# Attention's buffers in the place of the expert weights, 11 weight halves loaded early, and ScalarE's Gelu table asked for early

## The reference

```
x = layernorm(x + self_attention(x))        # 16 heads of 64, causal, with a projection
x = layernorm(x + cross_attention(x, ctx))  # 16 heads of 16, 77 context rows, one mask
x = layernorm(x + moe(x))
# moe: logits = x @ Wr.T; softmax; the two best of 8 experts, weights normalised;
#   for each expert e, in order: tokens of e up to a capacity of 1280;
#     the ones beyond it take the fallback FFN instead (fw1, fb1, fw2, fb2)
#   y += w * (gelu(x_e @ W1[e] + b1[e]) @ W2[e] + b2[e])   # exact gelu, 256 -> 1024 -> 256
```

## Time and profile before

| | |
|---|---|
| median of three runs | 1456.32 us |
| profiled execution | 1455.44 us, its span 1453.7 us |
| TensorE busy | 1288.9 us (89%), granted clock 0.96 on average |
| VectorE / ScalarE / GpSimd busy | 1081.1 / 922.0 / 731.8 us |
| attention block | 0 to 958.4 us |
| routing block | 958.4 to 1012.1 us |
| experts, final block | 1012.1 to 1401.6, 1401.6 to 1453.7 us |
| DMA | 208.96 MB, of which the 18 weight loads 18.9 MB |

### The profile page before, as it was taken

How to read it: one execution, slowest core, us unless ns; L and a number is a source line. 1 busy time by engine, 2 the same in 40 slices (tenths; PEclk the granted TensorE clock), 3 DMA queues, 4 the chain that set the end, 5 groups by cost and what they waited for, 6 DMA issues and landing times. The chain is left out here.

```text
span 1453.7 us, 47504 instructions
## 1 busy us (share of the span) xinstructions
PE 1288.9 (89%) x16821; PEld 1081.1 (74%) x16821; DVE 1081.1 (74%) x3112; ACT 922.0 (63%) x2383; POOL 731.8 (50%) x974
## 2 busy tenths in 40 slices
PE   4899999999999999999999998736999999999930
PEld 3788888887888888888888887513788888888820
DVE  4898899888888988988988988566455555555537
ACT  4677878777787887887888776304444444444436
POOL 4435666565566566566566453411243434444326
PEclk9999999999999999999999999965999999999975
DMA  9756767776776776767777654068233363333345
GB/s 242 132 101 137 160 148 188 166 155 150 200 158 144 204 154 156 180 172 154 159 197 160 130 112 76 23 253 338 61 70 80 102 164 75 74 74 75 70 157 201
DMA packets 292449, 208.96 MB, mean 144 GB/s; under 512 B 218782, under 2 KB 249630, under 8 KB 289792
## 3 DMA queue, kind: packets, MB, share of 16 engines
q1 hardware_dynamic: 278784, 180.87, 52.2%
q0 software_dynamic: 7136, 18.76, 4.5%
q10 hardware_dynamic: 6304, 6.29, 1.5%
HBM read 93.79 MB, written 65.93 MB: 110 GB/s over the span
## 5 line engine op out<-in xcount | busy, mean ns | idle before, releaser
L1784 PE MATMUL ps_e<-xt,wres 128*128 128x128 f16 x3408 | 343.4, 220 | 6.1 <-DMA xt<-xg 5.1
L1784 PEld LDWEIGHTS ps_e<-xt,wres 128*128 x3408 | 284.9, 98 | 78.3 <-issue 6.8
L1848 ACT ACTIVATE act_g<-ps_e,b 128x128 f32<-128x128 f32 x568 | 161.8, 368 | 208.6 <-PE ps_e L1784 208.6
L1791 PE MATMUL ps_e<-wres,g_hi 128*128 x568 | 214.6, 379 | 0.8 <-DVE g_lo L1871 0.8
L753 ACT ACTIVATE probs<-st_k,nmax 128x128 f32<-128x128 f32 (+1 forms) x512 | 202.3, 452 | 17.3 <-DVE nmax L1003 17.3
L1751 POOL DMA_INDIRECT z_scr<-e_y,dst_i x71 | 85.1, 1198 | 210.2 <-DVE e_y L1862 206.9
L1003 DVE CUSTOM_DVE_ANT_0 st_k<-ps,causal 128x128 f32<-128x128 f32 (+1 forms) x512 | 160.7, 351 | 31.9 <-ACT probs L753 16.5
L760 ACT ACTIVATE pt_hi<-ps 128x384 f16<-128x384 f32 x256 | 124.9, 488 | 59.1 <-PE ps L460 57.1
L1320 POOL TENSOR_TENSOR o_st<-o_norm,o_st 128x256 f16<-128x256 f32 x128 | 86.0, 672 | 149.7 <-ACT o_st L768 149.5
L1793 PE MATMUL ps_e<-wres,g_lo 128*128 x568 | 154.9, 273 | 0.0
L1008 DVE TENSOR_TENSOR pt_lo<-ps,pt_hi 128x384 f16<-128x384 f32 x256 | 140.9, 550 | 16.8 <-ACT pt_hi L760 15.6
(11 more groups left out here) (285 smaller groups left out, 3981.7 us busy)
## 6 DMA issues: line engine op xcount, KB each, us to landing
k_pair<-k_pair SPq DMA_DIRECT2D x96, 256.0 KB, 6.4
st_p<-in_moe_w SPq DMA_DIRECT2D x24, 768.0 KB, 6.7
w_scr<-st_p SPq DMA_DIRECT2D x24, 768.0 KB, 5.0
wres<-w_scr SPq DMA_DIRECT2D x18, 1024.0 KB, 22.7
v_scr<-v_tok SPq DMA_DIRECT2D x32, 512.0 KB, 4.3
v_pos<-v_scr SPq DMA_DIRECT2D x64, 256.0 KB, 6.1
q_st<-st_q SPq DMA_DIRECT2D x64, 128.0 KB, 2.8
z_scr<-zero SPq DMA_DIRECT2D x32, 256.0 KB, 5.2
```

What stands on the lines that cost most here:

```text
L1784: last = mm(out, w(c * FF + f * P, b, P), xt[:, t % X_BUFS, a, c], start=(m == 0), stop=(m == 5))
L1791: mm(out[:, 0:2 * D], g_hi[:, t % G_BUFS, f], w(KC * FF + f * D, 0, 2 * D), start=(f == 0), stop=False, skip_group_check=True)
L1848: nc.scalar.activation(act_g[:, k % 2, f], ps[:, 3 + 2 * (k % 2) + f // 4, (f % 4) * P:(f % 4 + 1) * P], ACT.Gelu, bias=bias[:, f:f + 1], ...
```

## The change

- The tensor wres (18 halves of 8 KB a partition, WSIZE = 4096 float16) is allocated before attention and stays. Attention's large buffers become views of it. In halves 0 to 10 (FRONT = 11) lie wqk (0, 1), wv (2), stage_p (3, 4), k_pair (5, 6), q_st (7), v_tok (8) and wp (9, 10); behind half 10 lie, by `kept`, w2, stage, stage_x, probs, o_st and o_t, which are in use to the end of attention.
- SP's queue in attention gets the loads of halves 0 to 10, in three parts: 0 to 4 in step 31, once all pieces are in w_scr and all fills are done; 5 to 8 in step 32, once all self-attention scores are computed and the last values have been stored; 9 and 10 once the last projection is done. The routing block loads halves 11 to 17.
- Attention's filler matmul reads w2["q"], since wv may be overwritten by then.
- ScalarE's queue of the experts block begins with one activation with Gelu on a single column, whose result is unused.

```diff
--- before.py
+++ after.py
@@ -57,6 +57,7 @@
 PAIRS = H // 2
 
 ZERO_STEPS = TILES
+FRONT = 11
 V_LOADS = 2
 
 V_FILLS, K_FILLS = 3, 4
@@ -77,10 +78,27 @@
         return ctx.enter_context(nc.semaphore(name))
 
 
-    wqk = {n: sb("w2_" + n, [P, 2, KC, PAIRS, 2, HS], F16) for n in "qk"}
-    wv = sb("wv_pair", [P, 2, KC, H * HS], F16)
-    wp = sb("proj_pair", [P, 2, H, D], F16)
-    w2 = {n: sb("xw_" + n, [P, 2, KC, D], F16) for n in ("q", "k", "v", "o")}
+    wres = keep["wres"]
+    taken = [FRONT * WSIZE]
+
+    def early(first, n, dims, **sizes):
+        return wres[:, first * WSIZE:(first + n) * WSIZE].rearrange("p (%s) -> p %s" % (dims, dims), **sizes)
+
+    wqk = {n: early(at, 1, "k c i x d", k=2, c=KC, i=PAIRS, x=2) for at, n in enumerate("qk")}
+    wv = early(2, 1, "k c n", k=2, c=KC)
+    stage_p = wres[:, 3 * WSIZE:5 * WSIZE].bitcast(F32).rearrange("p (h d) -> p h d", h=H)
+    k_pair = early(5, 2, "s l a t i", s=2, l=2, a=2, i=PAIRS)
+    q_st = early(7, 1, "s g a t i", s=2, g=2 * GROUPS, a=2, i=PAIRS)
+    v_tok = early(8, 1, "s h k d", s=2, h=H, k=2)
+    wp = early(9, 2, "k h d", k=2, h=H)
+    expert_rows = weight_rows(io)
+
+    def kept(n, dt, dims, **sizes):
+        at = taken[0]
+        taken[0] += n * (2 if dt is F32 else 1)
+        return wres[:, at:taken[0]].bitcast(dt).rearrange("p (%s) -> p %s" % (dims, dims), **sizes)
+
+    w2 = {n: kept(2 * KC * D, F16, "k c d", k=2, c=KC) for n in ("q", "k", "v", "o")}
     wr = sb("wr", [P, KC, E], F32)
     proj_b = sb("proj_b", [P, D], F32)
     ident = keep["ident"]
@@ -95,9 +113,8 @@
 
 
 
-    stage = {n: sb("st_" + n, [P, KC, D * 4], F32) for n in "vkq"}
-    stage_p = sb("st_p", [P, H, D], F32)
-    stage_x = {n: sb("st_x" + n, [P, KC, D], F32) for n in ("k", "v", "q", "o")}
+    stage = {n: kept(KC * D * 4, F32, "c n", c=KC) for n in "vkq"}
+    stage_x = {n: kept(KC * D, F32, "c n", c=KC) for n in ("k", "v", "q", "o")}
     ld = {n: sem("ld_" + n) for n in ("v", "k", "q", "p", "x")}
     s_small, s_hi, s_lo, s_const = sem("s_small"), sem("s_hi"), sem("s_lo"), sem("s_const")
 
@@ -127,20 +144,17 @@
     x_nat = sb("x_nat", [P, 2, D], F32)
     x_hi = sb("x_hi", [P, 2, KC, P], F16)
     x_lo = sb("x_lo", [P, 2, KC, P], F16)
-    q_st = sb("q_st", [P, 2, 2 * GROUPS, 2, GTOK // 2, PAIRS], F16)
     q_low = stage["q"][:, 0, 0:P * PAIRS // 2].bitcast(F16).rearrange("p (b t i) -> p b t i", t=GTOK // 2, i=PAIRS)
-    k_pair = sb("k_pair", [P, 2, 2, 2, P, PAIRS], F16)
-    v_tok = sb("v_tok", [P, 2, H, 2, HS], F16)
     v_pos = sb("v_pos", [P, 2, 2 * GROUPS, 1 + 2 * HS], F16)
     nmax = sb("nmax", [P, 2, 2], F32)
     masked = stage["k"][:, 0, 0:2 * 384].rearrange("p (g n) -> p g n", g=2)
-    probs = sb("probs", [P, 2, 384], F32)
+    probs = kept(2 * 384, F32, "g n", g=2)
     rden = sb("rden", [P, 4], F32)
     pt_hi = sb("pt_hi", [P, 2, 384], F16)
     pt_lo = sb("pt_lo", [P, 2, 384], F16)
     o_norm = sb("o_norm", [P, 2, 4, HS], F32)
-    o_st = sb("o_st", [P, 2, 2 * GROUPS, 2, HS], F16)
-    o_t = sb("o_t", [P, P, H], F16)
+    o_st = kept(2 * 2 * GROUPS * 2 * HS, F16, "s g k d", s=2, g=2 * GROUPS, k=2)
+    o_t = kept(P * H, F16, "t h", h=H)
     x_bias = sb("x_bias", [P, D], F32)
     y1 = sb("y1", [P, D], F32)
     y2 = sb("y2", [P, D], F32)
@@ -349,6 +363,11 @@
             sp.wait_ge(s_x2_lo, t + 1)
             sp.dma_start(io["pair_scr"][bass.ds(t * P, P), :], x2_pair[:, p].rearrange("p k d -> p (k d)")).then_inc(s_out_pair[p], 16)
 
+        def expert_weights(first, last):
+            for n in range(first, last):
+                at = slice(n * WSIZE, (n + 1) * WSIZE)
+                sp.dma_start(wres[:, at], expert_rows[:, at]).then_inc(keep["s_w"][n // 2], 16)
+
         def step(s):
             if s == -3:
                 load_x(0)
@@ -378,6 +397,16 @@
                 query_move(s + 1)
                 query_low_first(s + 1)
                 query_low_second(s + 1)
+            if s == TILES - 1:
+                sp.wait_ge(s_w_out, 16 * (PIECES + 1))
+                sp.wait_ge(s_fill, NF * TILES)
+                expert_weights(0, 5)
+            if s == TILES:
+                sp.wait_ge(s_scores, GROUPS * TILES)
+                sp.wait_ge(s_v_out, 16 * TILES)
+                expert_weights(5, 9)
+                sp.wait_ge(s_proj, TILES)
+                expert_weights(9, FRONT)
             if has(s - 2):
                 x2_out(s - 2)
                 pair_out(s - 2)
@@ -405,7 +434,7 @@
 
             if t == TILES - 1:
                 for _ in range(n):
-                    mm(ps_a[0], ident16[:], wv[:, 0, 0, 0:512], start=True, stop=True)
+                    mm(ps_a[0], ident16[:], w2["q"][:, 0].rearrange("p c d -> p (c d)"), start=True, stop=True)
 
         def fill(t, j):
             p = t % 2
@@ -1526,10 +1555,9 @@
     @block.sync
     def _(sp):
 
-        for e in range(NE):
-            for k in range(2):
-                at = slice((2 * e + k) * WSIZE, (2 * e + k + 1) * WSIZE)
-                sp.dma_start(keep["wres"][:, at], weight_rows(io)[:, at]).then_inc(s_w[e], 16)
+        for n in range(FRONT, 2 * NE):
+            at = slice(n * WSIZE, (n + 1) * WSIZE)
+            sp.dma_start(keep["wres"][:, at], weight_rows(io)[:, at]).then_inc(s_w[n // 2], 16)
         sp.dma_start(keep["b1"][:], io["b1T"]).then_inc(keep["s_b"], 16)
         sp.dma_start(keep["b2"][:], io["b2"].rearrange("(a n) -> a n", a=1).partition_broadcast(P)[:, 0, :]).then_inc(keep["s_b"], 16)
 
@@ -1724,6 +1752,7 @@
     s_share = sem("e_share")
     chosen = sb("e_chosen", [P, TILES, E], F32)
     moved = sb("e_moved", [P, TILES], F32)
+    unused = sb("e_unused", [P, 1], F32)
     block = ctx.enter_context(nc.Block())
 
     def expert_of(eng):
@@ -1837,6 +1866,7 @@
     @block.scalar
     def _(act):
         expert = expert_of(act)
+        nc.scalar.activation(unused[:], keep["neg_half"][:], ACT.Gelu)
         act.wait_ge(keep["s_b"], 32)
         for k in range(N):
             if k >= 2:
@@ -2013,11 +2043,11 @@
         }
         for n in ("s_b", "s_x2_in"):
             keep[n] = ctx.enter_context(nc.semaphore(n))
+        keep["wres"] = sb("wres", [P, NE * 2 * WSIZE], F16)
         keep["s_w"] = [ctx.enter_context(nc.semaphore("s_w%d" % e)) for e in range(NE)]
         with ExitStack() as phase:
             attention_block(nc, phase, io, keep)
         with ExitStack() as phase:
-            keep["wres"] = phase.enter_context(nc.sbuf_tensor("wres", [P, NE * 2 * WSIZE], F16))
             keep["xg"] = phase.enter_context(nc.sbuf_tensor("xg", [P, X_BUFS, 2 * D], F16))
             keep["hot"] = phase.enter_context(nc.sbuf_tensor("r_hot", [P, 2, TILES, E], F32))
             keep["over"] = phase.enter_context(nc.sbuf_tensor("r_over", [P, E, TILES], F32))
```

## The result

The changed kernel runs in 1471.80 us (median of 4 runs, 1468.10 to 1474.65), the kernel before in 1456.99 us on the same chip (4 runs, 1455.64 to 1457.85). The ratio is 1.0097 [1.0080, 1.0114]: slower, by 14.8 us between the medians. The forecast was 1455.2, with a range of 1452.9 to 1457.0; the result lies outside it, on the side that had 0.09.

What follows compares the result with a forecast made beforehand. TensorE was taken to run through from the first expert tile, so an earlier start reaches the end in full; 0.94 us (table) plus 0.2 us (change of block) made 1.14, from 1456.32 to 1455.2 us, range 1452.9 to 1457.0.

Steps and rivals of the forecast that it cites:

- Part 4: Attention's tail: the early weight loads, their new waits and the buffers' other addresses cost 0.
- full-load stretch: Attention with DMA at 0.99 and 362 GB/s: TensorE busy 2.00 of 2 us, VectorE 1.97, so heavy traffic costs 0.
- Part 1: Routing block: moving 11 weight halves out takes away 27.5 us of loading that nothing waited for, direct worth 0.
- Part 2: Change of block from routing to experts: lighter DMA traffic gains 0.2 us, with ends of 0 and 2.0.
- rival A: Change of block: the gathers' landing holds it, gain 1.3 to 2.0 us, in all 1453.8 us; chance 0.22.
- theory (b): Change of block: a fixed wait behind GpSimd's last instruction holds it; only the gathers' issue can shrink, at most 0.43 us.
- Part 3: Start of the experts: the early Gelu table load removes TensorE's wait for g_lo, 0.94 us, lower end 0.
- 48th matmul: First expert tile: ScalarE's second four tiles need it, at some 1018.9, so TensorE would not wait for g_lo.
- B: First expert tile: TensorE's clock stays up, on top of the gathers' earlier landing, 1.8 us more, 1452.0 us; chance 0.06.
- C: Change of block and first tile: nothing gained, gap fixed and another wait replaces g_lo, 1456.3 us; chance 0.14.
- D: Attention's tail: an instruction refill stands behind queued weight bursts, priced at 4 us slower, 1460.3 us; chance 0.10.

Runs made afterwards that it cites:

- e2: Kernel before with its separate DMA-touched buffers (stage, stage_p, stage_x, q_st, k_pair, v_tok) shifted by 32 bytes: 1475.32 us, ratio 1.0114.
- e5: Changed kernel with 96 bytes a partition ahead of wres, so that it begins at a multiple of 128: 1456.44 us, ratio 0.9990 to the kernel before.
- e11: Kernel before with only the three staging buffers st_v, st_k and st_q shifted by 32 bytes: 1469.21 us, ratio 1.0075.
- e13: Changed kernel, wres still 32 bytes off, with q_low as its own tensor at a multiple of 128: 1460.01 us, ratio 1.0011 to the kernel before.
- e15: Kernel before without its 24 weight pieces and with the three staging buffers shifted by 32 bytes: 1447.35 us, ratio 0.9931.
- e14: Kernel before without its 24 weight pieces (no load, split or store; experts' output wrong): 1447.48 us, ratio 0.9932.
- e6: Kernel before with q_st alone shifted by 32 bytes: 1456.18 us, ratio 0.9989.
- e3: Changed kernel with all 18 weight halves loaded in the routing block as before: 1475.89 us, ratio 1.0102 to the kernel before.
- e8: Changed kernel with wres at a multiple of 128 and no wait for GpSimd's DMAs at the routing block's end: 1456.46 us, ratio 0.9982 to the kernel before.
- e10: Kernel before with v_tok alone shifted by 32 bytes: 1458.96 us, ratio 1.0007.
- e1: Changed kernel with 32 bytes a partition ahead of wres and 32 behind, so wres begins 64 bytes beside a multiple of 128: 1473.72 us, ratio 1.0095 to the kernel before.
- e4: Kernel before with the added Gelu activation alone: 1457.98 us, ratio 0.9988.
- e16: Changed kernel with wres and also x2, x2_pair, ctx_t and xg at multiples of 128: 1458.14 us, ratio 0.9993 to the kernel before.

## Why the prediction was wrong

**The step that failed** stands in Part 4: "buffers at other addresses change no instruction's size: 0, with no row that would put a bound on it other than the full-load stretch below". The size is indeed the same: packets of each size class (292449, of which 218782 under 512 B) and bytes are equal in both profiles. The time of one is not. The two moves out of q_low went from 2.4 to 3.0 us and from 2.9 to 3.6, the piece behind them from 6.7 to 7.3, ScalarE's wait for pieces from 10.3 to 25.4 us, TensorE's for ScalarE from 7.7 to 20.4. That is +12.7 us of waits on the engine that sets the end, out of the 18.65 by which this execution was late at tile 31's load; 14.8 is the difference of the medians. The full-load stretch could not bound it: it shows that busy DMA engines leave TensorE and VectorE at work, and says nothing on how long one DMA takes or who waits for it. The prediction admitted an unknown without a bound and then put it at 0 and into no rival; the row that showed how little room there was, ScalarE's 12 waits for pieces already in the kernel before, was not read.

The links are not equally well shown. That addresses alone do it: shown (e2, e5). That the source of the low moves carries nearly all: shown (e11, e13). That the pieces are needed for it: shown by e15 beside e14. The order piece, ScalarE, TensorE is read from the waits of before, changed, e5, e11 and e13, in which the three numbers rise and fall together; that the slow move is what makes the piece behind it late rests on this, and no run moves a piece's place in the queue. Why q_st's shift, which slows the other two moves by 0.4 and 0.6 us, costs nothing (e6), is argued only: the move that lands last is not slowed by it, and the piece is not late (6.6 us). That TensorE's clock fell in 800 to 820 us is seen in the changed kernel's profile, and how much of the 14.8 us goes with it in other executions is open. Why a read from such an address takes longer stays open.

**Part 4, the loads themselves**, at 0: right. e3 has none of them and the same tail (22.01 against 21.98), and e5, which has them all, has the median of the kernel before. The tail's 1.64 us go with TensorE's clock, which was low in some stretches of the changed kernel (the columns are those of the earlier trace rows):

```profile
904.00:906.00 2.00, 1.38 (x20) 1.17 (x19) 1.97 (x8) 1.59 (x6) 1.07 (x2) 1.00 0.47 90
906.00:908.00 2.00, 1.52 (x9) 1.42 (x10) 1.60 (x6) 1.76 (x4) 0.61 (x1) 0.66 0.08 13
908.00:910.00 2.00, 2.00 (x19) 1.87 (x18) 1.89 (x7) 0.77 (x2) 0.00 (x0) 0.50 0.79 120
910.00:912.00 2.00, 1.22 (x19) 0.81 (x18) 1.34 (x4) 1.79 (x5) 0.67 (x1) 0.99 0.96 285
```

The clock (third column from the end; 0.50 is 1.2 GHz) falls ahead of 910.85, where the first early load is issued. A second dip comes at 914 to 918. The profiles of e3, e8 and e10 show two such dips and tails of 22.01, 21.94 and 22.01 us, e1 and e11 show one and 20.99 and 20.95; those of before and of e5 show 1.00 throughout and 20.34 and 20.38. So it comes and goes in kernels that gain and that lose, with early loads and without. One size in Part 4 was wrong without effect: the issue of five halves kept SP for 2.62 us and not for 6.4, and that of seven for 3.43; the 22.90 us for 18 are no rate for a few.

**Part 1**, the 11 halves out of the routing block, at 0: right; tok_i came 44.29 us after the block's start, as before.

**Part 2**, the change of block: the value of 0.2 us was wrong, its upper bound of 2.0 held, and rival A had the right size. I took theory (b), a fixed wait behind GpSimd, because of the 3.1 us at the experts' end. The runs show 9.07 to 9.34 us from tok_i to the transposes with all 18 halves in the block and 7.88 to 7.95 with seven: 1.3 to 1.4 us, which is the difference of the gathers' landing, 4.1 against 2.7. The fourth gather of the changed kernel, issued at 1027.82, was there at 1030.5 if it too took the 2.7 us, and the release at 1031.03 came as near behind it as before (1011.6 and 1012.09). The fillers do not set it: they ended 0.67 us ahead of it in the changed kernel and 0.31 to 1.05 us ahead in the others with seven halves, while from the fourth gather's issue to the transposes it is 3.14 to 3.21 us in all of them. The prediction's own rows had the answer: at attention's end the last store landed at 956.27 + 1.7 = 957.97, 0.5 us ahead of the next block and not the 0.3 of the text, the same 0.5 as here. The wait at the experts' end is a different one, and I had read a rule of one place into another. What waits for the landing stays open, since the drain that e8 leaves out is not it; and no run slows the gathers without loading the DMA engines, so that load delays the change of block in some other way, by the same 1.4 us, is not excluded.

**Part 3**, the table: predicted 0.94 us, found 0.1 (e4) and nothing in the changed kernel (+0.20). Only 0.2 us of the wait of 0.9 us went. The term that failed is the 48th matmul, taken at 4.0 us behind the first, "by 12 to 13 matmuls per us at the low clock". The counts in such rows take in matmuls that began before the stretch and were still in flight, so they are no pace. In e4 ScalarE's second four activations, which need the 48th, began 5.12 us behind the first matmul (1019.58 and 1014.46), in the changed kernel 5.44 (1039.27 and 1033.83). With that the split ended in e4 at 1022.78, when TensorE was already through its 96 matmuls (1022.38), and another 0.43 us passed before it went on. So the table had hidden a wait for TensorE's own slow first tile. The clock level, from stretches of the changed kernel:

```profile
1038.00:1039.00 1.00, 1.00 (x12) 1.00 (x11) 0.00 (x0) 0.20 (x1) 0.00 (x0) 0.50 0.00 0
...
1040.00:1041.00 1.00, 1.00 (x22) 1.00 (x20) 0.49 (x1) 0.41 (x2) 0.00 (x0) 1.00 0.58 119
```

After its first expert matmul at 1033.83 it ran at the low level for some 5.9 us. In e1 that was some 3.2 us: the clock fell only at 1035.2, 0.2 us ahead of the first expert matmul at 1035.4 and after 2.9 us without a matmul, and was back at 1.00 from 1039. TensorE had no wait for g_lo there, and the stretch to the final block took 385.94 us, 0.75 less than before; e16 (385.96) and e8 (386.27) have some 3 us at the low level and no such wait either. In e5, with the same table edit and the clock low from the start, the wait was 1.1 us and the stretch 386.82. So what the edit brings hangs on where the clock stands at the change of block; this is read from the profiles, and no run tried it by itself. The Trainium skill, "ScalarE: Activation LUTs", section "What ACT_TABLE_LOAD costs", puts the load of a table at some 1283 ns and a drain that goes with every switch at some 1380 ns more; the 1.28 us of the load agree, and in the rows above the activation follows 0.01 us behind the load, so that no such drain shows there.

**Rivals.** B came true in part in e1, e8 and e16, for 0.4 to 0.75 us of its 1.8 (a price that rests on the same misread counts as the 48th matmul), but not in the changed kernel; C did not. D had the right sign and the wrong mechanism: the late instruction was to stand behind a burst in attention's tail, but the kernel was late before any burst. No rival of mine had the addresses. The mark set for D, attention ending later than 958.4 by more than 0.5 us, was passed, at 978.79, and would by itself have pointed to D; only the issue time of the load ahead of the bursts cleared it.

The sum as it came out for e5, which has the change without the shift: 1.4 us for the gathers (9.34 to 7.93) and nothing for table and clock in its own profile (386.82 against 386.69), up to 0.75 in the profiles where the clock fell late; against 1.14 predicted and 1.6 measured between medians, which its interval doesn't tell from 0. That 1.14 lies near this is luck: the larger of its two terms brought almost nothing, and the smaller was 1.2 us short.

## What to carry to other kernels

When a buffer becomes a view of another, its address is part of the change: write down each buffer's offset within the partition and compare it with the one before, above all for the sources of small DMAs, and pay the 96 bytes if it is off. A cost that no row bounds is not 0; look for who waits for that queue already, since 12 waits of ScalarE for one kind of DMA mean that 0.6 us more of it may cost 10. And when attention, or any long stage, ends late, look first at the last mark ahead of the suspected edit: it may have been late by then.

## What the hardware showed that I had not expected

- The small moves within SBUF were slower in every run in which their source did not begin at a multiple of 128 bytes within the partition. A low move takes 16 runs of 128 bytes (8 tokens by 8 pairs in float16) from each of 64 partitions; one such move went from 2.4 to 2.8 us and the next from 2.9 to 3.6 with a shift of 32 bytes (e11), with equal packet counts. 64 bytes off cost as much in the whole kernel as 32 (e1). No other offset of the source was tried.
- A shifted destination slows two of the three moves too, 2.4 to 2.8 and 2.4 to 3.0 us (e6, with the first one's source shifted as well), but not the third, the second low move (2.9 in both). By the program's addresses, the two write runs of 128 bytes that begin 128 bytes beyond a multiple of 256 and, once shifted, cross the next one; the third writes runs that begin at a multiple of 256 and cross none. All runs here fit that (e13 too: 2.9, 3.0 and 2.9), but none tested it. The moves of keys (6.5 and 6.7 us against 6.6 and 6.9 in the changed kernel) and the key copy (3.1 in both) hardly notice.
- The Trainium skill, "DMA: Bandwidth & Descriptors", section "Specifications", wants at least 512 B in a transfer for full rate. Both kernels have the same 218782 packets under 512 B, so that row holds for both kernels alike and doesn't tell them apart; the start address does.
